# A two-block transformer stack: another order of each engine's instructions in the self and cross attention tiles

## What is computed

```python
ln_out = _ln(hidden_states, ln_w, ln_b)
q = _ln(_fp8_linear_pertensor(ln_out, wq, ...))      # 16 heads of 128
k = _ln(_fp8_linear_pertensor(ln_out, wk, ...))      # 8 groups of 128
v = _fp8_linear_pertensor(ln_out, wv, ...)
core = _gqa(q, k, v)                                  # "self"
qx = _ln(_fp8_linear_pertensor(ln_out, wqx, ...))
kx, vx = jnp.split(jnp.einsum('bsi,oi->bso', cond, w_kv_x), 2, axis=-1)
xout = _gqa(qx, _ln(kx), vx)                          # "cross"
catq = _div_clamp_fp8(jnp.concatenate([core, xout], axis=-1), proj_smooth)
return jnp.einsum('bsi,oi->bso', catq, wproj) * (proj_in_scale * proj_w_scale)
```

## Time and profile before

| | us |
|---|---|
| median of three runs | 708.07 |
| profiled execution | 705.51 |
| span of its trace | 703.4 |
| iterations 0 to 14 (204.5 to 537.5 in the trace) | 333.0 |
| TensorE busy over the span | 600.8 |
| VectorE busy over the span | 512.2 |

### The profile page before, as it was taken

One profiled execution on the slowest core, in us unless ns is written; L12 is line 12 of the kernel. 1 busy time (PEld: TensorE's weight loads), 2 busy tenths in 40 slices (PEclk: granted clock), 3 DMA queues, 4 the chain that ended last, 5 costly groups with the idle time before them and its releaser, 6 DMA issues.

```text
span 703.4 us, 10642 instructions
## 1 busy us (share of the span) xinstructions
PE 600.8 (85%) x3735; PEld 481.7 (68%) x3738; DVE 512.2 (73%) x951; ACT 378.1 (54%) x666; POOL 363.0 (52%) x299
## 2 busy tenths in 40 slices
PE   3696986579578799999999778899888989999995
PEld 2463433344367678887788768788777878888885
DVE  5679787589148889999988778888898764433332
ACT  1444767666278466665667555656566424433321
POOL 2321175000265775777667865666675743755521
PEclk9987998789799999999999989999999999999999
DMA  7850221003433003103147122122220100311001
GB/s 261 295 200 0 91 89 60 31 30 140 106 115 120 25 7 120 31 3 119 31 150 255 61 85 82 27 65 75 77 75 16 46 1 1 89 46 31 1 1 60
DMA packets 44563, 54.86 MB, mean 78 GB/s; under 512 B 8416, under 2 KB 30816, under 8 KB 44512
## 3 DMA queue, kind: packets, MB, share of 16 engines
q1 hardware_dynamic: 44512, 54.20, 23.5%
HBM read 41.60 MB, written 12.58 MB: 77 GB/s over the span
## 4 chain that ended last, share of the span: by engine, by line
PE 42%; DVE 16%; issue 9%; POOL 3%; ACT 2%; DMA 1%; SPq 1%; DVEq 0%; POOLq 0%; ACTq 0%
PE g_proj L2125 7%; PE g_proj L2049 6%; PE g_scores L2083 4%; DVE g_yb L1665 4%; PE g_turn L2072 3%; PE g_op L2107 2%; PE g_proj L457 2%; PE g_op L472 2%; PE g_proj L458 2%; PE g_op L474 2%; PE g_proj L459 2%; PE g_op L473 2%; DVE g_ve L1626 2%; POOL g_rs L1519 2%; DVE g_qn L1639 2%
## 5 line engine op out<-in xcount | busy, mean ns | idle before, releaser
L1519 POOL TENSOR_TENSOR g_rs<-g_ve,neg_half 128x4 f32<-128x4 f32 x80 | 84.9, 1065 | 49.8 <-DVE g_ve L1626 49.8
L2049 PE MATMUL g_proj<-w_hi,g_xqc 128*128 128x512 f32 x192 | 86.5, 450 | 9.0 <-POOL g_xqc L1513 6.0
L1535 POOL TENSOR_TENSOR g_cat<-g_yb,g_kb 128x1024 fp32r<-128x1024 bf16 x32 | 68.4, 2137 | 47.1 <-DVE g_yb L1681 47.1
L2049 PE MATMUL g_proj<-w_lo,g_xqc 128*128 128x512 f32 x192 | 79.7, 415 | 0.0
L2072 PE MATMUL g_turn<-ident,g_qn 128*128 128x128 f32 x384 | 60.4, 286 | 20.6 <-DVE g_qn L1639 10.5
L1843 ACT ACTIVATE g_sq<-g_proj 128x512 f32<-128x512 f32 x80 | 47.6, 595 | 46.8 <-PE g_proj L2049 43.9
L500 POOL TENSOR_TENSOR m_h_lo<-m_h,m_h_hi 128x512 fp32r<-128x512 f32 x32 | 41.4, 1296 | 60.2 <-ACT m_h_hi L487 60.2
L1626 DVE TENSOR_REDUCE g_ve<-g_sq 128x4 f32<-128x516 f32 x80 | 54.2, 681 | 24.6 <-ACT g_sq L1843 24.3
L2083 PEld LDWEIGHTS g_scores<-g_qkT 128*128 128x128 f32 x512 | 61.4, 195 | 10.6 <-issue 10.0
L2072 PEld LDWEIGHTS g_turn<-ident,g_qn 128*128 128x128 f32 x384 | 45.8, 146 | 32.3 <-DVE g_qn L1639 13.0
L2083 PE MATMUL g_scores<-g_qkT 128*128 128x64 f32 x512 | 62.5, 276 | 6.0 <-DVE g_ex L1649 6.0
(11 more groups left out here) (232 smaller groups left out, 1698.2 us busy)
## 6 DMA issues: line engine op xcount, KB each, us to landing
kvx_rows<-f_kept SPq DMA_DIRECT2D x32, 256.0 KB, 2.4
g_ksq<-kvx_rows SPq DMA_DIRECT2D x8, 512.0 KB, 4.4
g_kraw<-kvx_rows SPq DMA_DIRECT2D x16, 256.0 KB, 3.4
g_v<-kvx_rows SPq DMA_DIRECT2D x8, 512.0 KB, 4.7
m_raw<-in_L_W SPq DMA_DIRECT2D x16, 256.0 KB, 3.0
c_raw<-in_L_wqT SPq DMA_DIRECT2D x4, 512.0 KB, 9.1
f_w_ctx<-in_L_wkvxT SPq DMA_DIRECT2D x4, 512.0 KB, 7.7
x_raw<-in_L_wqxT SPq DMA_DIRECT2D x4, 512.0 KB, 3.8
```

The costliest lines, as they stand in the source:

```text
L1519: G.tensor_tensor(rs[:, at % 2, :], ve[:, at % 2, :], k["half"][:, 0:4], ALU.pow).then_inc(q["rs_done"], 1)
L1535: G.tensor_tensor(cat[:, h].rearrange("p h (b s) -> p b h s", b=2), yb[:, h, :].rearrange("p (b h s) -> p b h s", b=2, s=SEQ), kb[:, h, :] ...
L2049: last = T.matmul(bank(n, i)[:], xqc[:, n % 2, view * KT + c_, :], w[:, c_, :], start=c_ == 0 and part == 0, stop=c_ == KT - 1 and part == 1)
```

## The change

The body of the loop is written in another order on all four engines. No operation is added or taken away, no wait inside a step is changed; one wait written into the loop (`x_done` ahead of `moe.turn`) moves with its step. The code ahead of and behind the loop is the same. In short, for a self iteration:

- TensorE: `turn(n, 5)` ahead of `scores(n, 0)`; `project(m, 4)` ahead of `turn(m, 1)` and `attend(n, 0)`; `turn(m, 2)` ahead of `project(m, 5)`; `project(m, 7)` last.
- VectorE: `less_max(n, 1)` ahead of `sums(m, 1)`; `ctx.low` or `ctx.mean`, then `scale(m, 1)`, then `add_x`, then `key_sums`; `scale(m, 2)` ahead of `sums(m, 3)`; `clip(n, 0)` right behind `unload(n, 0)`; `scale(m, 4)` behind `lift(n, 0)`; `scale(m, 5)` between `unload(n, 1)` and `clip(n, 1)`.
- ScalarE: `key_squares(n)` first; `exponent(n, 0)` between the two squares; in iteration 0 the four weight pieces earlier; `keep_pT(n, 0)` still behind `keep_qk(m, 0)`, `keep_pT(n, 1)` behind `square(m, 5)`.
- GpSimd: `ctx.centre` ahead of `rstd(m, 2)`; `copy_tile` behind `normalise(n, 1)`; `key_rstd(n)` between the two `fp8`; in iteration 0 the third `own_out.low` behind `rstd(1, 0)` and the fourth last.

In a cross iteration: TensorE starts with `project_context(m, 1)` and `turn(n, 4)`, and does `turn(m, 0)` ahead of `scores(n, 1)` and `output`, and `moe.turn` ahead of `turn_p(n, 1)`; ScalarE does `square(m, 1)` and `scale(m, 0)` ahead of the three `keep_qk(n, ...)`, in iterations 7 and 8 both `ctx_out.high` ahead of `keep_qk(m, 0)`, and `keep_pT(n, 1)` and `scale(m, 3)` last.

The diff, with lines that did not change left out where they only separate:

```diff
@@ -1555,35 +1555,35 @@
...
         rstd(m, 0)
+    if n == 0:
+        own_out.low(pool, 2)
+    if n in TOKENS:
+        moe.rstd(pool, TOKENS[n])
     rstd(m, 1)
-    if n < LAST - 1:
-        copy_tile(n + 2)
     normalise(n, 0)
+    if n in (1, 3, 5):
+        ctx.centre(pool, (n + 1) // 2)
     rstd(m, 2)
+    if n in MATRIX:
+        moe.low(pool, MATRIX[n])
+    if not cross(m):
+        rstd(m, 3)
     if n in (TILES - 1, TILES):
...
         ctx_out.low(pool, 2 * (n - TILES + 1) + 1)
-    if n in TOKENS:
-        moe.rstd(pool, TOKENS[n])
-    if not cross(m):
-        rstd(m, 3)
     normalise(n, 1)
+    if n < LAST - 1:
+        copy_tile(n + 2)
     rstd(m, 4)
-    if n in MATRIX:
-        moe.low(pool, MATRIX[n])
-    if n in (1, 3, 5):
-        ctx.centre(pool, (n + 1) // 2)
     rstd(m, 5)
-    if n == 0:
-        own_out.low(pool, 2)
+    fp8(n, 0)
+    if not cross(n):
+        key_rstd(n)
     if n - 1 in TOKENS:
         moe.rest(pool, TOKENS[n - 1])
-    fp8(n, 0)
+    fp8(n, 1)
     if n == 0:
         own_out.low(pool, 3)
-    fp8(n, 1)
-    if not cross(n):
-        key_rstd(n)
 
...
@@ -1710,65 +1710,65 @@
...
     sums(m, 0)
-    sums(m, 1)
     total(n, 0)
     less_max(n, 1)
-    scale(m, 1)
+    sums(m, 1)
     if n % 2 == 0:
...
         ctx.mean(dve, (n + 1) // 2)
+    scale(m, 1)
+    if n > 0:
+        add_x(n - 1)
     key_sums(n)
...
     total(n, 1)
-    if n > 0:
-        add_x(n - 1)
+    scale(m, 2)
     sums(m, 3)
-    scale(m, 2)
     unload(n, 0)
+    clip(n, 0)
     sums(m, 4)
-    clip(n, 0)
     power(n, 0)
-    scale(m, 4)
     sums(m, 5)
     lift(n, 0)
+    scale(m, 4)
     unload(n, 1)
+    scale(m, 5)
     clip(n, 1)
-    scale(m, 5)
     power(n, 1)
...
     less_max(n, 0)
-    if n - 1 in TOKENS:
-        moe.keep_logits(dve, TOKENS[n - 1], proj[OUT_BANK])
-    if n == TILES - 1:
-        key_sums(n)
     sums(m, 1)
...
         token_moments(TOKENS[n])
+    if n - 1 in TOKENS:
+        moe.keep_logits(dve, TOKENS[n - 1], proj[OUT_BANK])
+    sums(m, 2)
     total(n, 0)
-    sums(m, 2)
+    scale(m, 1)
     less_max(n, 1)
-    scale(m, 1)
     scale(m, 2)
+    if n == TILES - 1:
+        key_sums(n)
     total(n, 1)
...
         moe.normalise(dve, TOKENS[n])
+    add_x(n - 1)
     sums(m, 4)
-    add_x(n - 1)
-    sums(m, 5)
     unload(n, 0)
     clip(n, 0)
+    sums(m, 5)
     power(n, 0)
+    lift(n, 0)
     scale(m, 4)
-    lift(n, 0)
     unload(n, 1)
+    scale(m, 5)
     clip(n, 1)
-    scale(m, 5)
     power(n, 1)
...
@@ -1911,65 +1911,65 @@
...
     m = n + 1
+    if n == 0:
+        own_out.high(act, 2)
+    key_squares(n)
     square(m, 0)
+    exponent(n, 0)
+    if n == 0:
+        split_query(0)
     square(m, 1)
-    exponent(n, 0)
-    key_squares(n)
     scale(m, 0)
...
     if n == 0:
-        split_query(0)
+        own_out.high(act, 3)
     square(m, 2)
...
     keep_qk(m, 1)
-    if n == 0:
-        own_out.high(act, 2)
     square(m, 4)
+    keep_qk(m, 2)
     scale(m, 3)
+    square(m, 5)
     keep_pT(n, 1)
-    square(m, 5)
-    keep_qk(m, 2)
+    keep_v(m, 0)
+    keep_qk(m, 3)
     if n in (1, 3, 5):
         split_query((n + 1) // 2)
-    if n == 0:
-        own_out.high(act, 3)
-    keep_qk(m, 3)
-    keep_v(m, 0)
     keep_qk(m, 4)
...
     m = n + 1
+    square(m, 1)
+    scale(m, 0)
+    if n in (TILES - 1, TILES):
+        ctx_out.high(act, 2 * (n - TILES + 1))
     if cross(n):
...
         key_squares(n)
-    square(m, 1)
+    square(m, 2)
     exponent(n, 0)
-    square(m, 2)
-    scale(m, 0)
-    exponent(n, 1)
-    if n in (TILES - 1, TILES):
-        ctx_out.high(act, 2 * (n - TILES + 1))
     if n in MATRIX:
         moe.high(act, MATRIX[n])
-    keep_qk(m, 0)
-    square(m, 4)
-    keep_pT(n, 0)
-    square(m, 5)
     if n in (TILES - 1, TILES):
         ctx_out.high(act, 2 * (n - TILES + 1) + 1)
+    keep_qk(m, 0)
+    exponent(n, 1)
+    keep_pT(n, 0)
+    square(m, 4)
     keep_qk(m, 1)
-    keep_pT(n, 1)
-    scale(m, 3)
+    square(m, 5)
     keep_qk(m, 2)
...
         moe.keep(act, TOKENS[n], proj[OUT_BANK])
+    keep_pT(n, 1)
+    scale(m, 3)
 
...
@@ -2143,8 +2143,8 @@
...
     m = n + 1
+    turn(n, 5)
     scores(n, 0)
-    turn(n, 5)
     project(m, 0)
...
@@ -2152,45 +2152,45 @@
...
     turn(m, 0)
+    project(m, 3)
     turn_p(n, 0)
-    project(m, 3)
+    project(m, 4)
     turn(m, 1)
     attend(n, 0)
-    project(m, 4)
+    turn(m, 2)
     project(m, 5)
-    turn(m, 2)
     turn_p(n, 1)
...
     attend(n, 1)
-    project(m, 7)
     turn(m, 3)
     turn(m, 4)
+    project(m, 7)
 
...
     m = n + 1
-    scores(n, 0)
+    project_context(m, 1)
     if cross(n):
         turn(n, 4)
-    turn(n, 5)
     if n - 1 in TOKENS:
         moe.logits(pe, TOKENS[n - 1], proj[OUT_BANK])
-    project_context(m, 1)
+    scores(n, 0)
+    turn(n, 5)
     project_context(m, 2)
+    turn(m, 0)
     scores(n, 1)
     output(n - 1)
-    turn(m, 0)
+    turn_p(n, 0)
     project_context(m, 4)
-    turn_p(n, 0)
-    project_context(m, 5)
     turn(m, 1)
     attend(n, 0)
+    project_context(m, 5)
     turn(m, 2)
+    if n in TOKENS:
+        pe.wait_ge(q["x_done"], n)
+        moe.turn(pe, TOKENS[n], proj[OUT_BANK])
     turn_p(n, 1)
...
     turn(m, 3)
-    if n in TOKENS:
-        pe.wait_ge(q["x_done"], n)
-        moe.turn(pe, TOKENS[n], proj[OUT_BANK])
 
```

## The result

The changed kernel takes **689.07 us** (688.03 to 690.41), the kernel before 708.24 us beside it: a ratio of 0.9726, 95% interval 0.9692 to 0.9759. The forecast was 695.6 us with a range of 688 to 706, so the time lies in the range, at its low end, and it is the time that rival B gave (689). The profiled execution took 688.03 us, 17.5 us less than that of before.

The account below looks back on a forecast made before the run. TensorE and VectorE, taking turns in being last, bound the middle; the named wait was TensorE's for VectorE's `scale(n, 5)`, 10.5 us. Terms summed to -12.5, so 693.0 profiled, plus 2.56 gives 695.6 us; range 688 to 706.

Parts of the forecast that it names:

- rival B: Whole kernel: iteration 7 costs nothing, middle periods of 22.2, iterations 10 to 14 at 19.3 each; 689 us, chance 0.14.
- the last step: Whole kernel: adds 2.56 us, the median's excess over the profiled time, taking 693.0 to 695.6 us.
- the terms of a cross iteration: Iterations 10 to 14: 17.3 of work, 1.6 of waits, 0.6 of switches and margin, given as 19.6 us each.
- the end piece of the middle: Middle: the piece beside its five `output` to `output` periods, 11.4 us before and 12.3 after.
- Middle: To the end of iteration 6: `scale(m, 5)` ahead of the clip cuts TensorE's idle time; period 22.5, -2.7 us.
- The 0.3 us for the clip beside `normalise`: Middle: `clip(n, 0)` meets GpSimd's `normalise(n, 1)`, costing between nothing and 1.1 us a period; 0.3 taken.
- Head: Iteration 0 to the end of `output(0)`: stalled instructions go, `output(0)` ends at 237.4 against 243.1; -5.7 us.
- Iteration 7: Gets worse: waits of 2.2 at `turn(8, 0)`, 2.7 at `turn_p(7, 0)`, 2.3 at `turn_p(7, 1)`, lower clock 1.2; +2.5 us.
- Iteration 8: The 3.12 us wait and most lower clock go, `turn(8, 5)` waits 1.5 for `keep_qk(8, 3)`; -3.0 us.
- Iterations 10 to 14: Waits for `scale(n, 5)` go, the one ahead of `attend(n, 1)` grows to 1.4; 19.6 each against 20.3, -3.3 us.
- A: Middle and cross tiles gain nothing, as other engines' chains fill each gap; only head and passage count: 701.9 us, chance 0.22.
- C: Cross tiles: ScalarE ends last, at 1.8 us more per iteration over eight, giving +4.6, 712.7 us; chance 0.12.

Follow-up runs that it names:

- a_clip0_late: The changed kernel with `clip(n, 0)` put back behind `sums(m, 4)` on VectorE in the self iterations; 690.74 us.
- a_pool_before: The changed kernel with GpSimd's order of the kernel before throughout, the other engines keeping the new order; 702.1 us.
- a_clip_first_self: The changed kernel with one swap undone, `clip(n, 1)` ahead of `scale(m, 5)` again in the self iterations; 700.32 us.
- a_high_late: The changed kernel with `ctx_out.high` on ScalarE moved from behind `scale(m, 0)` to behind `exponent(n, 0)` in iterations 7 and 8; 684.98 us.
- cross_only: The kernel with the old order in iterations 0 to 6 and the new order in 7 to 14; 699.06 us.

## Why the prediction was right, and where it was off

The sign, the range and the mechanism of the middle held; the point was 6.5 us too high. 5.0 us of that are terms of the loop and of what lies around it, as the table shows; the other 1.5 come from the last step: I added 2.56 us to get from the profiled execution to the median, and for the changed kernel the two differ by 1.04. Two sums of the working were a little off: the terms of a cross iteration add to 19.5, not 19.6, and the end piece of the middle before was 11.2 us (370.6 less 359.4), not 11.4.

*Middle, -2.7 forecast, -2.6 measured.* The wait at `turn(n, 5)` is 0.15 (0.4 forecast), the one at `turn_p(n, 1)` 0.26 to 1.15 (0.6 forecast), the periods 21.97 to 22.92 with a mean of 22.5. The 0.3 us for the clip beside `normalise` stood for nothing that `a_clip0_late` could find. What the working had wrong though its sum was right: it counted `ctx.centre` at nothing, as lying in a gap. That is true of its new place. Its old place, beside the new order of VectorE, costs 2.6 us in each of the iterations 1, 3 and 5 (24.62, 25.48 and 25.51 us against 21.97, 22.92 and 22.91), lower clock included: 7.8 of the 13 us that `a_pool_before` lost.

*Head, -5.7 forecast, -4.6 measured.* `scores(1, 1)` no longer waits, `output(0)` waits for the fourth `own_out.low`, as forecast, and ended at 236.5. That is 0.9 earlier than the 237.4 of the forecast, because the loop began 2.0 earlier; in the loop's own time it came 1.1 later. The reason given was half right: the stall goes by GpSimd's order (3.81 us of it come back in `a_pool_before`), not by `scale(1, 5)`.

*Iteration 7, +2.5 forecast, +0.1 measured.* This term failed most. Of its three waits, 2.2 at `turn(8, 0)`, 2.7 at `turn_p(7, 0)` and 2.3 at `turn_p(7, 1)`, the trace shows 1.59, none and 1.76. The second is missing for two reasons in this trace (timeline of the kernel after, and its DMA issues with the median from issue to landing, as in the earlier trace rows):

```profile
369.24 1.06 ACT L225 ACTIVATE w_hi<-x_praw 128x1024 fp32r<-128x1024 f32 x1 [2.12 <-DMA x_praw<-in_L_wprojT]
...
373.35 1.04 POOL L1529 TENSOR_TENSOR g_ex<-g_ex,g_rc 128x512 f32<-128x512 f32 x1 [5.52 <-DVE g_rc L1659]
...
374.72 0.60 PE L2092 MATMUL g_turn<-ident,g_ex 128*128 128x128 f32 x4
```

```profile
x_praw<-in_L_wprojT SPq DMA_DIRECT2D x4, 512.0 KB, 7.8
```

ScalarE got past the wait for `x_praw` 7.8 us into the iteration and not 9.7, so `normalise(7, 0)` ended 13.0 us in, not 15.0. And TensorE came to `turn_p(7, 0)` 1.0 later than forecast (13.3 in, not 12.3), because `output(6)` ran at the lower clock and took 5.1 us instead of 3.83; for that clock 1.2 us had been put in the sum, so it paid for part of itself.

The first of these is luck of this execution. `a_clip0_late` has the same order from here on; there the transfers took 9.5 us in the median, and ScalarE got past the wait 8.1 us after the first was issued, for 6.3 in the trace above. Even so `turn_p(7, 0)` did not wait, since the clock was low for 7.0 us and `output(6)` took 6.2, and the two periods from `output(5)` to `output(7)` came to the same 48.6 us. In `a_clip_first_self`, with this order too, `output(6)` ran at full clock: there the three waits of the forecast stand, but as 1.60, 1.60 and 1.97 us and not 2.2, 2.7 and 2.3, and the two periods are 47.8 us. So two steps of this term failed: its waits were too long by 2.0 us together, and the wait at `turn_p(7, 0)` and the lower clock were added, 2.7 and 1.2, where lower clock in `output(6)` hides that wait. `a_high_late` shows that the wait of 2.12 us for `x_praw` is on the path all the same, by way of `turn_p(7, 1)`.

*Iteration 8, -3.0 forecast, -2.5 measured.* The 3.12 us are gone, and `turn(8, 5)` waits 1.42 us for `keep_qk(8, 3)` (1.5 forecast). *Iteration 9* as forecast.

*Iterations 10 to 14, -3.3 forecast, -4.9 measured.* The one wait left is the one forecast, 1.30 us at `attend(n, 1)` (1.4 forecast). The 0.3 us an iteration that were too much are waits: 1.6 us were in the sum and 1.30 are there. That the periods come down at all needs VectorE's new order, which the forecast did not name: with the old one they are 20.9. Which of its moves does it was not separated; the trace points to `unload(n, 0)` ahead of `sums(m, 5)`.

*Outside the loop, 0 forecast, -2.8 measured.* The code is the same. The loop began at 204.5 us before and at 202.5 after; ahead of it the clock was low in two pieces, 10.2 and 3.4 us, before and in one of 13.7 after. `a_high_late`, which is the changed kernel in all that runs before iteration 7, shows the two pieces again, and its `output(0)` starts at 235.0, 2.3 us later than that of the changed kernel (232.7); `cross_only`, with the old order at this place, shows the one piece. So these 2.0 us are chance of one execution and not the change's. They do not explain the 1.5 us by which the last step missed: a profiled execution that is 2 us short by chance would lie further below the median, not nearer to it. The 0.8 us behind the loop are left open, too.

Of the rivals, A is refuted, C did not come (ScalarE is last at `attend`, but with 1.3 us, where 0.69 at `attend`, 0.76 and 0.56 at two turns stood before), and B had the two places right at which my sum was short, iteration 7 and the cross tiles; its middle of 22.2 a period did not come. That its 689 is the measured median is luck: it gave 19.0 us to the loop, where the loop gained 14.7, and the other 4.3 are the 2.8 outside it and the 1.5 of the last step. In the loop the forecast's 12.5 was nearer. Its chance of 0.14 was too low all the same.

## What to carry to other kernels

A reordering across engines is worth what its parts do together: here the swap that removes the named wait gained nothing alone (708.5 us), and the parts taken out singly (this swap, GpSimd's order, VectorE's order in the cross tiles) cost 11, 13 and 16 us where the whole gained 19. Over the iterations, by contrast, the two halves of the change added. Cost a move at its new place and at its old place beside the other engines' new orders, and look for GpSimd's wide operations beside VectorE instructions that work in SBUF alone; what VectorE reads from PSUM can go there. A wait taken away is worth its length only if no other engine is within that length of being last (4.4 us of waits gave 1.4). Lower clock that happens to follow a wait comes on top (2.4 us of waits went and 4.1 us came back), but it does not follow every wait and should not be counted on. And compare two traces first where their code is the same: here that part alone differed by 2 us.
